# Window attention of a fused network: heads split over the two halves of the partitions, one product for a pair's values, weighing over 128 rows

## The reference

```python
xw = windows of 7x7 pixels of x       # 8 x 8 = 64 windows, 49 pixels each
xc = jnp.concatenate([wt, xw], axis=-1)                 # a learned token ahead: 50 tokens
qkv = jnp.einsum('oc,bcn->bon', w_qkv, xc)              # 16 heads of 32
q, k, v = jnp.split(qkv, 3, axis=1)
dots = jnp.einsum('bhid,bhjd->bhij', q * scale, k)      # 50 x 50 for each head
attn = jax.nn.softmax(dots, axis=-1)
out = jnp.einsum('bhij,bhjd->bhid', attn, v)
```

## Time and profile before

| | us |
|---|---|
| time, median of 3 runs | 10540.76 |
| lowest and highest run | 10527.25, 10558.55 |
| span of the profiled execution, first to last instruction | 10494.0 |
| PE busy in it | 8547.4 (81%) |
| DVE busy | 7405.7 (71%) |
| ACT busy | 3939.7 (38%) |
| POOL busy | 202.9 (2%) |

### The profile page before, as it was taken

How to read it: one execution, slowest core, us unless ns; L and a number is a source line. 1 busy time by engine, 2 the same in 40 slices (tenths; PEclk the granted TensorE clock), 3 DMA queues, 4 the chain that set the end, 5 groups by cost and what they waited for, 6 DMA issues and landing times.

```text
span 10494.0 us, 288483 instructions
## 1 busy us (share of the span) xinstructions
PE 8547.4 (81%) x124030; PEld 4636.8 (44%) x124030; DVE 7405.7 (71%) x8856; ACT 3939.7 (38%) x6092; POOL 202.9 (2%) x254
## 2 busy tenths in 40 slices
PE   6478888887887888788888878888887888888887
PEld 5324444353443435344353534435353443435444
DVE  2487777668677776867677687767768776786763
ACT  0034434253443425334342533434353343434332
POOL 0000000000000000000000000000000000000000
PEclk7579898998989899898899889898998988899898
DMA  4001101111110111111011111101111110111101
GB/s 108 6 12 36 45 21 46 33 38 36 41 45 20 43 36 37 37 40 45 19 45 36 35 39 33 52 20 43 32 41 39 31 52 20 44 29 42 41 22 52
DMA packets 230327, 391.83 MB, mean 37 GB/s; under 512 B 25200, under 2 KB 166480, under 8 KB 221776
## 3 DMA queue, kind: packets, MB, share of 16 engines
q1 hardware_dynamic: 229008, 372.66, 12.9%
HBM read 192.47 MB, written 130.55 MB: 31 GB/s over the span
## 4 chain that ended last, share of the span: by engine, by line
PE 59%; DVE 22%; issue 10%; ACT 6%; DMA 1%; DVEq 0%; SPq 0%; POOL 0%; ACTq 0%; POOLq 0%
PE ps L879 10%; PE ps L683 7%; PE ps L748 7%; DVE arena L1692 4%; PE ps L781 4%; PE ps L979 4%; PE ps L705 3%; PE ps L797 3%; PE ps L969 3%; PE ps L756 3%; DVE arena L1747 3%; PE ps L770 2%; PE ps L702 2%; DVE arena L1787 2%; DVE arena L1669 1%
## 5 line engine op out<-in xcount | busy, mean ns | idle before, releaser
L879 PE MATMUL ps<-arena,ident 64*64 64x512 f32 x5600 | 1768.6, 683 | 702.8 <-DVE arena L1692 699.5
L881 PE MATMUL ps<-arena,ident 48*64 48x512 f32 x5600 | 1776.9, 684 | 36.8 <-issue 36.8
L1692 DVE TENSOR_TENSOR arena<-arena 112x2560 f32<-112x2560 f32 x560 | 1578.3, 2819 | 108.7 <-PE ps L881 102.1
L879 PEld LDWEIGHTS ps<-arena,ident 64*64 64x64 f32 x5600 | 491.4, 150 | 1757.3 <-issue 1747.3
L748 PE MATMUL ps<-arena,wqk 128*128 128x400 f32 x2048 | 933.5, 576 | 198.6 <-DVE arena L1796 126.2
L683 PE MATMUL ps<-vp,convw 128*128 128x448 f32 x2016 | 819.1, 549 | 23.6 <-ACT vp L1298 23.6
L1781 DVE COPY arena<-ps 128x400 f32<-128x400 f32 x512 | 292.8, 572 | 732.4 <-PE ps L748 731.1
L1675 DVE TENSOR_TENSOR arena<-arena 112x576 f32<-112x576 f32 x1008 | 764.2, 758 | 34.9
L1219 ACT ACTIVATE arena<-ps 112x864 f32<-112x864 f32 x224 | 199.5, 890 | 1527.7 <-PE ps L705 1523.0
L1787 DVE TENSOR_REDUCE arena<-ps 128x16 f32<-128x800 f32 x512 | 504.7, 986 | 345.0 <-PE ps L770 341.5
L797 PE MATMUL ps<-arena 64*64 64x33 f32 x32768 | 644.0, 230 | 106.8 <-issue 59.1
(11 more groups left out here) (287 smaller groups left out, 12889.5 us busy)
## 6 DMA issues: line engine op xcount, KB each, us to landing
windows_out<-arena SPq DMA_DIRECT2D x1024, 100.0 KB
arena<-windows_out SPq DMA_DIRECT2D x224, 256.0 KB, 4.0
arena<-windows_out SPq DMA_DIRECT2D x224, 192.0 KB, 3.4
arena<-in_wqk SPq DMA_DIRECT2D x16, 2048.0 KB, 8.3
arena<-in_x_t SPq DMA_DIRECT2D x16, 1568.0 KB, 10.7
arena<-in_x SPq DMA_DIRECT2D x16, 1568.0 KB, 7.8
arena<-arena SPq DMA_DIRECT2D x32, 784.0 KB
out_x<-xb SPq DMA_DIRECT2D x112, 224.0 KB, 2.0
```

The lines of the kernel that those rows point to most:

```text
L879: nc.tensor.matmul(ps[half, 3, :], ident[0:SLOT, 0:SLOT], prod[0:SLOT, ring(c, dy), dx, :], start=(s < 2), stop=(s >= TAPS - 2), skip_grou ...
L881: mm = nc.tensor.matmul(ps[half, 4, :], ident[SLOT:PT, SLOT:], prod[SLOT:PT, ring(c, dy), dx, :], start=(s < 2), stop=(s >= TAPS - 2), ski ...
L1692: V.tensor_tensor(prod[0:PT, ring(c, dy), :, :].rearrange("p k (n e) -> p k n e", e=CG), taps.to_broadcast([PT, SHIFTS, N64, CG]), for_tap ...
```

## The change

The layout of the attention's intermediate tiles is changed. The two halves of the partitions now hold the two halves of the heads, not the two windows of a pair. With that, the transposed exponentials have the keys of both windows on their 128 rows. The values of a pair come from one product of 128 x 128 weights and 512 moving columns and stand in `v_sb` block by block: rows 0 to 63 (window 0) in its first block, rows 64 to 127 (window 1) in its second, zeros elsewhere. Each `weigh` product then has 128 rows, 64 weight columns and 66 moving columns (two blocks of 33), and there are 16 of them, not 32. ScalarE copies the values by two instructions of 64 partitions. GpSimd zeroes all of `v_sb` and then writes the columns of ones. VectorE's division and SyncE's DMAs follow the layout. `heads()` goes away.

```diff
@@ build: the values tile
-        v_sb = [cv(NH * VD).rearrange("p (k d) -> p k d", k=NH) for _ in range(2)]
+        v_sb = [cv(2 * NH * VD).rearrange("p (k w d) -> p k w d", k=NH, w=2) for _ in range(2)]
@@ SyncE windows_out
-                for wi in range(2):
-                    w = 2 * s + wi
-                    sp.dma_start(wfd[w:w + 1, :, :].rearrange("a n c -> (a n) c"),
-                                 o_sb[s % 2][wi * SLOT:wi * SLOT + NTOK, :]).then_inc(wf_out[s % 2].sem, 16)
+                for hh in range(2):
+                    sp.dma_start(wfd[2 * s:2 * s + 2, :, hh * 256:(hh + 1) * 256].rearrange("w n c -> n w c"),
+                                 o_sb[s % 2][hh * SLOT:hh * SLOT + NTOK, :].rearrange("p (w c) -> p w c", w=2)
+                                 ).then_inc(wf_out[s % 2].sem, 16)
@@ GpSimd zero_windows
                 for u in range(2):
-                    ins = nc.gpsimd.memset(v_sb[u][:, :, DH:], 1.0)
-                ins.then_inc(l2_z.sem, 1)
-                for u in range(2):
                     nc.gpsimd.memset(e_sb[u][:, :, NTOK:], 0.0).then_inc(l2_z.sem, 1)
-
+                own.turn(i, 3)
+                nc.gpsimd.memset(v_sb[0], 0.0)
+                own.step(nc.gpsimd.memset(v_sb[1], 0.0))
+                alone(pool)
+                for wi in range(2):
+                    half = slice(wi * SLOT, (wi + 1) * SLOT)
+                    for u in range(2):
+                        ins = nc.gpsimd.memset(v_sb[u][half, :, wi, DH:], 1.0)
+                    own.step(ins)
+                    alone(pool)
+                pool.sem_inc(l2_z.sem, 1)
@@ TensorE values
-                for wi in range(2):
-                    for hh in range(2):
-                        mm = nc.tensor.matmul(ps[hh * SLOT:(hh + 1) * SLOT, 4, wi * 256:(wi + 1) * 256],
-                                              xwb[b % 2][:, 2 * pr + wi, :], wv[:, hh * 256:(hh + 1) * 256],
-                                              start=True, stop=True, skip_group_check=True)
-                mm.then_inc(v_p.sem, 1)
+                nc.tensor.matmul(ps[:, 4, :], xwb[b % 2][:, 2 * pr:2 * pr + 2, :], wv[:, :], start=True, stop=True
+                                 ).then_inc(v_p.sem, 1)
@@ TensorE scores
-                for r, place, m in heads():
+                for kk in range(2):
                     for wi in range(2):
-                        w = (2 * pr + wi) * NTOK
-                        mm = nc.tensor.matmul(ps[wi * SLOT:(wi + 1) * SLOT, r, place * NTOK:(place + 1) * NTOK],
-                                              qk[b % 2][32 * r:32 * r + 32, m, w:w + SLOT],
-                                              qk[b % 2][32 * r:32 * r + 32, 4 + m, w:w + NTOK],
-                                              start=True, stop=True, skip_group_check=True)
+                        w, at = (2 * pr + wi) * NTOK, (2 * kk + wi) * NTOK
+                        for r in range(4):
+                            for hh in range(2):
+                                m = 2 * hh + kk
+                                mm = nc.tensor.matmul(ps[hh * SLOT:(hh + 1) * SLOT, r, at:at + NTOK],
+                                                      qk[b % 2][32 * r:32 * r + 32, m, w:w + SLOT],
+                                                      qk[b % 2][32 * r:32 * r + 32, 4 + m, w:w + NTOK],
+                                                      start=True, stop=True, skip_group_check=True)
@@ TensorE weigh
                     for hh in range(2):
-                        for wi in range(2):
-                            at = x8 * C + wi * SLOT
-                            mm = nc.tensor.matmul(
-                                ps[wi * SLOT:(wi + 1) * SLOT, 6 + hh, (kk * 4 + r) * VD:(kk * 4 + r + 1) * VD],
-                                et[u][hh * SLOT:(hh + 1) * SLOT, at:at + SLOT],
-                                v_sb[u][hh * SLOT:(hh + 1) * SLOT, wi * 8 + kk * 4 + r, :],
-                                start=True, stop=True, skip_group_check=True)
+                        at = x8 * C + hh * SLOT
+                        mm = nc.tensor.matmul(ps[hh * SLOT:(hh + 1) * SLOT, 6 + kk, r * 2 * VD:(r + 1) * 2 * VD],
+                                              et[u][:, at:at + SLOT],
+                                              v_sb[u][:, hh * 8 + kk * 4 + r, :, :].rearrange("p w d -> p (w d)"),
+                                              start=True, stop=True, skip_group_check=True)
@@ ScalarE values
-                nc.scalar.activation(v_sb[s % 2][:, :, 0:DH], ps[:, 4, :].rearrange("p (k d) -> p k d", k=NH), ACT.Copy
-                                     ).then_inc(v_s.sem, 1)
+                for wi in range(2):
+                    own_rows = slice(wi * SLOT, (wi + 1) * SLOT)
+                    ins = nc.scalar.activation(v_sb[s % 2][own_rows, :, wi, 0:DH],
+                                               ps[own_rows, 4, :].rearrange("p (k d) -> p k d", k=NH), ACT.Copy)
+                ins.then_inc(v_s.sem, 1)
@@ ScalarE windows: the wait for the zeroed tiles goes from its head to just before the first gather
-                act.wait_ge(l2_z.sem, l2_z.at(i))
...
+                act.wait_ge(l2_z.sem, l2_z.at(i))
                 gather(i, 0)
@@ VectorE normalise
-                V.tensor_tensor(o_sb[u].rearrange("p (a h d) -> p a h d", a=2, h=8), pv[:, :, :, 0:DH],
-                                rv.to_broadcast([C, 2, 8, DH]), ALU.mult).then_inc(o_s.sem, 1)
+                ins = V.tensor_tensor(o_sb[u].rearrange("p (w a r d) -> p a r w d", w=2, a=2, r=4),
+                                      ps[:, 6:8, 0:8 * VD].rearrange("p a (r w d) -> p a r w d", r=4, w=2)[:, :, :, :, 0:DH],
+                                      rec[u].rearrange("p (a r w d) -> p a r w d", a=2, r=4, d=1).to_broadcast(
+                                          [C, 2, 4, 2, DH]), ALU.mult)
+                ins.then_inc(o_s.sem, 1)
```

5 lines of the change are left out of this document (2 added, 3 removed).

## The result

| | before | after |
|---|---|---|
| median of the runs, us | 10547.25 | 10636.17 |
| lowest and highest run, us | 10527.25, 10558.55 | 10608.12, 10650.3 |
| ratio, 95% interval | | 1.0086 [1.0067, 1.0105] |
| span of the profiled execution, us | 10494.0 | 10606.3 |
| mean granted clock in it | 0.881 | 0.888 |

The changed kernel is slower by some 89 us between medians; 130 were forecast, and the time lies in the range. The two profiled spans differ by 112 us.

A forecast was written before the change was run, and what follows sets the result against it. TensorE was taken to bound most steps, tied with ScalarE's copy of the values. Terms 136 - 9 + 10 - 15 + 8 made +130 us on a 10494 span; with the runs' median, 10670 us, range 10520 to 10860.

The forecast's parts named there:

- What bounds the kernel: TensorE sets the pace in most steps; ScalarE's copy of the values ties with the second queries-and-keys product's weight load.
- Values on TensorE: Values product as two records of 512 columns takes 1.13 us for 1.08, +0.05 us for those who wait.
- Copy of the values: On ScalarE, each 64-partition copy takes as long as a full one, so the pair ends 0.48 us later.
- What it costs: Second queries-and-keys product is signalled 0.53 us later in 341 cases; three quarters of 181 us raw, +136 us.
- Mode of the array: Between values and queries and keys, same tile shape saves drain and load, 0.16 us a step; -9 us.
- Weighing: TensorE's 16 waves of 66 columns hide their weight loads; +0.02 us a step, +10 us.
- Rival A: Weight loads stay exposed in the weighing, 1.6 us for 1.14; +165 us on the forecast less its 10, 10825; chance 0.13.
- Fewer instructions: Weighing line's 59 us of unexplained waits, in 52 cases, shrink as half its records go; -15 us.
- Clock: TensorE's granted clock stays, though its share of waiting rises; 0, or some 73 us if 0.89 fell to 0.87.
- the +8 for the last steps: In steps 29 to 32, without queries and keys, the transposes wait for the copy; +8 us.
- B: Rival: two 64-partition copies take no more than one full copy, the drain's saving shows; faster, 10450; chance 0.13.
- C: Rival: later waits in the same step shrink by what TensorE loses, only 65 cases count; 10550; chance 0.14.

The follow-up runs named there:

- Run 12: Changed kernel with both copies of the values reading and writing rows 0 to 63, into the buffer's two blocks; one run, 10553 us.
- run 2: Changed kernel with one copy of all 128 rows into the first block, so rows 64 to 127 stand wrong; 0.9885 of before.
- run 1: Kernel before with only ScalarE's copy of the values cut into two instructions of 64 partitions; 1.0186 of before.
- run 4: Changed kernel with the values in four products of 256 columns on halves of the weight columns; 1.0065 of before.
- run 8: Changed layout with one copy, single-width buffer, weighing in 64 records on quarters, and values in four products of 64 weight columns; 0.9980 of before.
- run 5: Changed kernel with one copy, a single-width buffer and weighing on quarters in 64 records of 64 rows by 33 columns; 0.9989 of before.
- run 7: Kernel before with the copy cut by heads into two of 128 partitions and 256 elements from the same bank; 1.0021 of before.
- run 11: Kernel before with two copies both reading rows 0 to 63 and writing rows 0 to 63 and 64 to 127; one run, 10734 us.

## Why the prediction was right, point by point

The place and the sign were right, and the time lies in the range. That it lies near the forecast is in part luck: two terms were too small by 76 and by 95 us, with opposite signs.

*What bounds the kernel.* Right. The tie between the copy and the second product was the place; the copy moved by 0.6 us and TensorE with it.

*Values on TensorE.* Right: 1.12 us for 1.13.

*Copy of the values.* The mechanism was right and the size was off: "two such behind each other begin 0.48 us apart" was read from two copies that write the same 128 partitions, and these two write different ones. They begin about 0.61 apart (1.21 less 0.60). Run 12 has the case that I priced. The missing overlap is 0.11 us a pair by the medians of the starts (0.49 apart in run 12, 0.61 in the changed kernel), at most 448 x 0.11 = 49 us by that count; the spans of run 12 and of the changed kernel differ by 55 us, one execution each.

*What it costs.* +136 was forecast and 212 measured (run 2 to the changed kernel; 196 from before to run 1). Up to 49 of the difference of 76 is the missing overlap. The rest is in "I take three quarters": with the true pair the raw sum is 341 x (0.05 + 0.64) = 235 us, and 212 of it stayed, so VectorE took up little. The wait row alone grew by 203.5 us (49.0 to 252.5), and that of the transposes behind the same copy by 17.4 (27.5 to 44.9). 252.5 us in 325 cases also means 0.78 a case, where my mean was 0.53. The cases are of two kinds. All 65 waits of the kernel before (0.75 us on average) stand in steps where ScalarE loads a table of functions (ACT_TABLE_LOAD, 1.28 us) before its exponentials, so that the copy begins late. In the changed kernel 64 waits of 1.5 us, 97.6 us in all, stand behind such a load, and the other 261 last 0.59 on average. The prediction saw these 65 cases and not the load. Timeline of the changed kernel:

```profile
2324.80 1.28 ACT L1164 ACT_TABLE_LOAD   x1 [0.67 <-DVE arena L1794]
2326.09 0.87 ACT L1164 ACTIVATE arena<-arena 128x800 f32<-128x800 f32 x1
2326.87 1.20 ACT L1156 ACTIVATE arena<-ps 64x512 f32<-64x512 f32 x2
...
2328.12 0.94 PE L753 MATMUL ps<-arena,wqk 128*128 128x400 f32 x2 [1.50 <-ACT arena L1156]
```

*Mode of the array.* -9 was forecast, which is less than the runs can tell; no gain was seen, with (run 4) and without (run 8) the copy in the way. The queries and keys begin 0.96 us after the values for 1.01, so at most 0.05 us a step came of it, and nothing waits for that.

*Weighing.* Right, +0.01 us a step (1.15 for 1.14) for +0.02. Rival A is out: the Trainium skill, "TensorE: Matmul & The Clock Gate", Part 3, lets a load overlap only where the row group differs, and here all rows are used by each product; the trace disagrees, 0.060 us a wave for 0.055 by count.

*Fewer instructions.* This is the term that was mis-sized most: -15 forecast, some -110 measured (run 5 to run 2). I priced the stops by their own 59 us and took a quarter, and didn't ask what was short. It was the instructions themselves (run 5), of which a step now needs 0.90 packets for 1.19. The stops on this line went entirely ("issue" on all TensorE lines goes from 124 to 82 us), and with them pieces at half clock that followed them. One such piece in the timeline of the kernel before, which ends with the rows:

```profile
2246.69 1.11 PE L797 MATMUL ps<-arena 64*64 64x33 f32 x58
2251.18 0.43 PE L797 MATMUL ps<-arena 64*64 64x33 f32 x6 [3.37 <-issue]
2251.54 1.97 PE L756 MATMUL ps<-wv,arena 128*64 128x256 f32 x8
```

TensorE stands for 3.37 us in the middle of the weighing, and then the values take 1.97 us for 1.08 and the queries and keys 3.04 for 1.73: the half-clock step of the earlier trace rows follows such a stop, and I quoted it for the copy without asking what had slowed the clock. "*Clock*: 0" failed for the same reason, in the kernel's favour: the mean went from 0.881 to 0.888 although TensorE waits longer.

*The sum.* 212 for the copy, 110 back for the fewer records, and 12 (run 5, within its interval of nothing) for the rest make +90, where 89 was measured. That is no check, since the three are the steps from before over runs 5 and 2 to the changed kernel; run 1 is one, with 196 us for the copy alone. The forecast of 130 was nearer than its terms: 76 too little on the one (68, if the +8 for the last steps is counted with it) and 95 too little on the other.

*B and C.* B is out: a copy of 64 partitions takes 598 ns. C is out: the waits later in the step didn't shrink (119.9 for 126.2). That the copy is not made good later but a stop elsewhere is cured was in none of the rivals.

## What to carry to other kernels

Cutting one ScalarE instruction in two by partitions doubles its time, and if the halves write different partitions they don't even overlap: look who waits for it first, above all where a wait is a tie (the weight load released, the product just not). When TensorE stops for "issue" in short products, compare the end of the stop with the landing of its instruction packets: here it had run out of instructions. Such a stop can cost more than its row says, where work at half clock follows; fewer and longer records cured it here, at equal work. When a change has a dear part and a cheap part, measure each alone: the change as a whole costs 0.9%, its wide products without the second copy would gain 1.2%, and no version that puts all values in their places was found here that has the one without the other (the best of those, runs 5 and 8, are at 0.999 and 0.998, not told apart from before).

## What the runs showed of the hardware

- Two ScalarE copies from PSUM behind each other overlap by about 0.1 us when they write the same partitions (0.48 apart for 590 ns, run 12; 0.28 apart for 378 ns, run 7), and not when they write different ones (1.19 to 1.21 for the pair, runs 1, 11 and after). With different ones written, reading the same ones doesn't help (run 11).
- 16 waves of four products of 33 columns on quarters of the array, and 16 waves of two products of 66 columns on halves, take the same time (1.14 and 1.15 us), with loads of 64 columns for each.
- TensorE's stops for "issue" on the weighing line came with 64 records in 1.14 us (59.1 us in all, 52 times), hardly with 64 in 2.08 us, and not with 32 in 1.15 us. Every one of them ends 1.20 to 1.60 us after a 16 KB packet of instructions has landed, and 256 records to a packet lie between them (before, run 5): TensorE had no instructions left. Not every "issue" is such a stop: the 15 of the scores line (7.6 us in all) end 1.7 us or more after the last landing.
- ScalarE's load of a table of functions took 1.28 us, and every wait of TensorE for the copy in the kernel before stands behind one.
- Whether the second copy could go to GpSimd, or the values into a bank of their own in the changed kernel's order, wasn't tried.
